# New sequences of steps for all engines, TensorE's filler steps taken out, and SyncE's wait for scattered rows at every load

## The reference

```python
x = x + 0.5 * L0_ffn(layernorm(x))     # top-2 of 8 experts plus a shared one, swiglu
x = x + L0_attn(layernorm(x))          # linear attention, 32 heads, group norm
x = x + 0.5 * L0_ffn(layernorm(x))     # the same routed layer again
x = x + 0.5 * L1_ffn(layernorm(x))     # top-1 of 8 small experts, gelu
x = x + L1_attn(layernorm(x))          # gated recurrence, 8 heads, rope
x = x + 0.5 * L1_ffn(layernorm(x))
```

## Time and profile before

| | |
|---|---|
| median of 3 runs | 1516.47 us (1516.26 to 1516.67) |
| the profiled execution: span | 1515.8 us |
| TensorE busy | 1313.6 us, 87% |
| VectorE busy | 1153.5 us, 76% |
| ScalarE busy | 805.2 us, 53% |
| GpSimd busy | 672.4 us, 44% |
| mean granted TensorE clock | 0.950 of full speed |

### The profile page before, as it was taken

One profiled execution on the slowest core, in us unless ns is written; L12 is line 12 of the kernel. 1 busy time (PEld: TensorE's weight loads), 2 busy tenths in 40 slices (PEclk: granted clock), 3 DMA queues, 4 the chain that ended last, 5 costly groups with the idle time before them and its releaser, 6 DMA issues.

```text
span 1515.8 us, 42570 instructions
## 1 busy us (share of the span) xinstructions
PE 1313.6 (87%) x15621; PEld 1012.9 (67%) x15621; DVE 1153.5 (76%) x3632; ACT 805.2 (53%) x1302; POOL 672.4 (44%) x727
## 2 busy tenths in 40 slices
PE   1566987798978889888898899999999999999998
PEld 0344765576766777666676777777876776767776
DVE  5888788779756698788898587767688778877775
ACT  0344655436534556453566456767666546546662
POOL 0056637785557357767678433221433335210100
PEclk9978999899989999999999999999999988989999
DMA  9002313332143214221333221121110010000000
GB/s 284 0 29 76 104 52 105 90 87 71 52 116 100 66 52 113 70 69 53 107 91 96 71 77 44 40 58 46 43 37 17 22 33 25 17 24 2 9 16 23
DMA packets 128044, 94.30 MB, mean 62 GB/s; under 512 B 15723, under 2 KB 119302, under 8 KB 127590
## 3 DMA queue, kind: packets, MB, share of 16 engines
q1 hardware_dynamic: 108038, 54.17, 12.3%
q0 software_dynamic: 16384, 33.59, 7.6%
q10 hardware_dynamic: 3424, 3.81, 0.8%
HBM read 45.90 MB, written 45.61 MB: 60 GB/s over the span
## 4 chain that ended last, share of the span: by engine, by line
PE 54%; DVE 25%; issue 7%; POOL 6%; ACT 5%; DMA 1%; SPq 0%; POOLq 0%; DVEq 0%; ACTq 0%
PE bank L668 9%; PE bank L725 4%; POOL rows L1605 3%; PE bank L682 3%; PE bank L661 3%; PE bank L702 2%; POOL y_in L1622 2%; PE bank L752 2%; PE bank L530 2%; PE sums L899 2%; PE bank L882 2%; PE sums L913 2%; PE bank L489 2%; DVE heads_store L940 2%; DVE heads_store L1020 1%
## 5 line engine op out<-in xcount | busy, mean ns | idle before, releaser
L1622 POOL DMA_INDIRECT y_in<-ys,r_result x256 | 273.5, 1069 | 120.9 <-issue 69.7
L1605 POOL DMA_INDIRECT rows<-store,r_slot x256 | 264.0, 1031 | 108.9 <-issue 75.8
L668 PE MATMUL bank<-u_xp_odd,w_hi 128*128 128x128 f16 x1216 | 128.6, 224 | 6.9 <-ACT u_xp_odd L1391 6.7
L668 PE MATMUL bank<-u_xp_even,w_hi 128*128 128x128 f16 x1216 | 126.8, 221 | 4.8 <-ACT u_xp_even L1391 4.7
L661 PE MATMUL bank<-r_member,by_expert 128*128 128x512 bf16 x304 | 118.0, 388 | 8.9 <-ACT u_linear_even L1471 3.1
L668 PEld LDWEIGHTS bank<-u_xp_odd,w_hi 128*128 x1216 | 96.5, 100 | 32.4 <-issue 12.0
L668 PE MATMUL bank<-u_xp_odd,w_lo 128*128 128x128 f16 x608 | 117.8, 223 | 0.0
L668 PE MATMUL bank<-u_xp_even,w_lo 128*128 128x128 f16 x608 | 115.7, 220 | 0.0
L668 PEld LDWEIGHTS bank<-u_xp_even,w_hi 128*128 x1216 | 95.1, 98 | 30.1 <-issue 9.2
L1416 ACT ACTIVATE heads_store<-bank,b3s,sc 128x512 f32<-128x512 f32 x64 | 49.4, 775 | 72.3 <-PE bank L530 72.1
L530 PE MATMUL bank<-heads_store,w_hi 128*128 128x512 f16 x256 | 81.8, 403 | 3.8 <-ACT u_linear_odd L1471 1.4
(11 more groups left out here) (348 smaller groups left out, 3797.8 us busy)
## 6 DMA issues: line engine op xcount, KB each, us to landing
u_rows<-rows SPq DMA_DIRECT2D x304, 64.0 KB
ys<-u_y_even SPq DMA_DIRECT2D x38, 256.0 KB
ys<-u_y_odd SPq DMA_DIRECT2D x38, 256.0 KB
x<-x_dram SPq DMA_DIRECT2D x16, 256.0 KB, 7.3
rows<-store,r_slot POOLq DMA_INDIRECT x256
y_in<-ys,r_result POOLq DMA_INDIRECT x256
out_dram<-x SPq DMA_DIRECT2D x16, 256.0 KB
rows<-blank SPq DMA_DIRECT2D x48, 64.0 KB, 1.5
```

Of the source, the lines that this page charges most:

```text
L668: ins = pe.matmul(B[:, of_block[j]], of_expert(wp, e, 2 * part + which), s.xp[:, xp, of_block[j]], start=False, stop=(n == 2 and j == PER_ ...
L1605: pool.indirect_dma_start(row_dram[g], bass.IndirectOffsetOnAxis(route.slot[g][:, i, t:t + 1].bitcast(U32), 0), rows[:, groups[g].first * ...
L1622: pool.indirect_dma_start(fetch.y[i][:, t, k, :], None, y_dram[g], bass.IndirectOffsetOnAxis(route.result[g][:, k, t0 + t:t0 + t + 1].bitc ...
```

## The change

The five strings are replaced. Each has the same letters as before, as many times each, and so the same steps with the same work; only `z`, which stood 462 times in TensorE's string, now stands once, near the end. The first two lines of TensorE's string, before and after:

```diff
         turns = {
             "tensor": (
-                "aazzzzzzzzzzzzzzzzzzzzzzzzzzzzzzzzzzzzzzzzzzzzzzzzzzzzzzzzzzzabbzzzzzzzzbcczzcaabbcaaarrrrbbbcbbbccc"
-                "aaabbabbbaccczccaaarrrrrbbbcccbrrrbaaazzzzzzzzzzzzzzzzarrrrrbbbcccaccaaazzzzzzzzzzzzzzzzzzzuwrrrrrzz"
+                "acbarbabcacaababarbbbbccbarrrrcrarabccbbcbbaabbacrcrcccrababacbcarbrabararbrccacarbbrcrcuwururburwwcau"
...
+                "vvvolvovvllloloooolozlo"
             ),
```

The second edit is in `load_rows`:

```diff
                 firsts = load_numbers(route.row[l][g][0:1, PER_UNIT * u:PER_UNIT * (u + 1)], spare_at + (groups[g].blocks - 1) * BLOCK)
-                if u == 0:
-                    on.wait_ge(scattered[g], 16 * 2 * groups[g].tiles * (l + 1))
-                    on.wait_ge(cleared[g], 16 * (1 + E * (l + 1)))
+                on.wait_ge(scattered[g], 16 * 2 * groups[g].tiles * (l + 1))
+                on.wait_ge(cleared[g], 16 * (1 + E * (l + 1)))
                 if i >= 3:
```

More of the change, by code:

```diff
@@ L396, in build @@
[L396 to L400, removed]
+                "acbarbabcacaababarbbbbccbarrrrcrarabccbbcbbaabbacrcrcccrababacbcarbrabararbrccacarbbcrcuwrurburwwcau"
@@ new lines, in build @@
+                "rwucucwuurcwbucwwbuaububawrbcwuawccuwwwubaaucbaucbcraruwwawurwuarrwauuubwrucbaawaucrwrrwrwracrarraba"
+                "bcwacuwuurawabbaawracucurucrcwaawuubwwrruuawuararuwaucwbucawauwubawbubaruwrabucbcawubwucbcuaubcaabab"
+                "aarcrwwaucwbabbburcaacwcbaawbuawbawacurcacwwaawrruwaccwuuucwauauurawacurawwrarwaauwrwuwuwmuwwruuwuwb"
+                "bbrucwcuwaawuauwuwurbwuuwbuwbwwuubnwbcbwbuuubbbcaucwwcbucbcwcbwwabcbuwcbauubawrrcubwauwcwbacuuwcuaaa"
+                "cuburcaurbcwbccuwbawaabrwccwcbaaaabcuwbcrruwubbwcuwwuubcbcaabacrwccabumrabubacnwacwbcuburawubrbbacca"
@@ new lines, in build @@
+                "bcaacwubwurabucwaabwcuawbcbuaaawarbcrnbuccruabwwuubcbwcrbwacbubawccuwaruauwcbbcawaccrcbraurwabrcbcca"
+                "cawbrubcwauwbraabbauwuacrbcauawlbcwucbubrcuaacbabrwwabcwcwabuuucwarwbcaurcawucuwuwurcwuaurwwcuawrcwa"
+                "auucauauwmwwauruwuwuawwuwruwuuaawwuurmrmmuwmuwnmwnwmntnummttmwnmwutwmttnnwuuottttwutwuowtvwvmnvmuttu"
+                "vtvtmvwmwwnltummttunuvwlnwttnluuunvvmvtlltvnulwumttnmnwtnvmtlowwtuuuvvlwouovmwulvvnwowuuovtotwulnutu"
+                "wntllwowttttowlvvvmlvvwwumvuwnmwtuolouwomluonwmtoutowmuntmutwwttnutnwttmvwmtnomvltnmvntvvtnvttnmmtmt"
@@ L414, in build @@
[L414 to L417, removed]
+                "ababacbccaabraabbrbarbcabcrababccrwccbbacrabrbrcabrbcarcababcrcbabrrrccabrbcruacarrbacrbcbacruuruwwc"
@@ new lines, in build @@
+                "nnottonlffmfotttfftlntftmontfmotolnltmftffmmtotftnlmmtmnmfmfttmlfcftnntttlmanfomfftmoonffftnfnommtft"
+                "nnonbtfftfnlltntamltntmmllnttmofottmftoftlffolffntnlftfntftomfnfltffanlfnttnfmmmmtltnotofttmftnomnmn"
+                "cftttofntffftnflfltmnofmnfftlmftfftmflmtftntlffltoomltlttftlftfbotffmnttnolmlnfannnntltotnoofmmmtmol"
+                "obttmfofmtofttffoftttttblntnottlottltontttcotlltbtonotlalmtlotmtlobtlmntlntlttllttmmnoltcolomlltttoo"
+                "otcoolatloloootlonototlonmcoollb"
@@ L458, in build @@
+                "ulwuwuuuuouuwwwwwuwwwuluwuuwwuuwwwwwulwwuouwwuuuwuuuuwlowluwuwluoluowwluwlulowwuuwllwlwwwluowlooolwl"
+                "ouwlouoloouuwouoouuluowwwulwlooololoooloololloollloollooollllllloololollololllllollollollloolooooolo"
+                "oolooooo"
             ),
```

100 lines of the change are left out of this document (43 added, 57 removed).

## The result

The changed kernel takes 1414.18 us (median of 4 runs, 1407.98 to 1417.71); the kernel before, run beside it, takes 1516.57 us (1516.26 to 1521.25). The ratio is 0.9311, with a 95% interval of 0.9281 to 0.9342. So 102 us went away. 28 us had been predicted, and the range ended at 1462, 48 us above the result: the direction was right, the size far off.

What follows compares the result with a forecast made beforehand. Middle part taken as bound by waits between TensorE and VectorE, last part by TensorE itself. Terms -15 -10 -8 -6 +7 -3 +6 +1 = -28 us; 1515.8 - 28 + 0.7 = 1488.5 us, range 1462 to 1514.

Steps and rivals of the forecast that it cites:

- The fillers, -15 and -10 us: TensorE's filler matmuls taken out: 15 us gained in the last part, 10 us (of 0 to 23) in the middle part.
- The clock, +6 us: TensorE without fillers: 15 us more of half clock at 0.42 cost 6 us, range 0 to 40 us.
- the first rival: Without fillers TensorE falls to 1.2 GHz in the dense part too: slower, 1528 us; chance 0.15.
- TensorE's order, -8 -6 +7 us: Down projection (line 679) gains 8 us, row search (line 608) 6; new waits cost 7; bounds 21 worse to 30 better.
- The named waits: TensorE's waits at the down projection (line 679), 21.3 us, and at the row search (line 608), 9.1 us.
- VectorE's and ScalarE's orders: ScalarE's order: three table loads fewer, 4 us, hidden, so 0; VectorE's order has no term in the sum.
- New waits, 7 us: Waits that TensorE's new order brings and the trace cannot show: 7 us put against that order.
- The third rival: All fillers pay (45 us), waits on lines 679 and 608 (30 us) go with little new: 1464 us; chance 0.16.
- GpSimd, -3 us: GpSimd's first fetch of results comes after 86 scatters instead of 100: 3 us gained, of 0 to 8.
- SyncE, 0: SyncE's edited wait for scattered rows at every unit: six instructions carry it in both programs, so worth 0.
- clock and start: Clock term of 6 us, plus 1 us because the first chunk now meets half clock at the start.

## Why the prediction was wrong, step by step

The sum had 25 us for the fillers and 10 us for the sequences (-8 -6 +7 -3). Measured, taking the fillers out costs 7 us in the old sequences and gives 8 us in the new, and the sequences give 97 to 113 us (1520.1 to 1423.1 with fillers, 1527.7 to 1414.8 without).

- **The fillers, -15 and -10 us:** the step that failed first. Taken out by themselves they changed the time by +7 us (interval of the ratio 1.0015 to 1.0072). I argued that no idle time stood in front of the first matmul behind a run of fillers, so the run must be on the path. But the row shows only that this operand was ready by then; without the run the idle time came back elsewhere (after 60 us TensorE was idle 155 us before, 179 without fillers). Absent idle time behind a filler is no proof that its time can be gained.
- **The clock, +6 us:** for the fillers alone the first rival had the mechanism, but it paid for only part of what the fillers gave back. The granted clock fell from 0.950 to 0.925, half-speed time from 2 x 0.050 x 1516 = 152 to 2 x 0.075 x 1527 = 229 us; at the 0.42 worked out from the earlier trace rows that is an estimated 32 us. An estimated 45 us of fillers gone (at 0.109 us each), 32 us back by the clock and 23.5 us more idle time add up to the 11 us by which the profiled run without fillers is longer. But in the whole change the term has the other sign. The 39 us of busy time between the two kernels without fillers are clock, since the matmuls are the same: by the windows' clocks half-speed time fell by some 87 us, an estimated 37. With its gaps closed TensorE was granted 0.947 and 0.959 in two profiled runs with one filler left.
- **TensorE's order, -8 -6 +7 us:** the step that failed in size, by a factor of ten. The named waits went about as told (the prediction had 13 us left at line 679, there are 8; the row search kept one wait of 2.0). The error is in what a wait is worth: I priced the microseconds in TensorE's own waits on two lines, bounded by their total of 30. The down projections' spacing alone is worth 93 us in the changed kernel, of which 38 are waits at their own line; the rest comes back at other lines, through what VectorE and ScalarE then do later, and as a lower clock.
- **VectorE's and ScalarE's orders:** VectorE's had no term at all, and ScalarE's had 0, from its table loads. These are the two that cost 420 and 247 us when they alone are put back, in the longer session. The prediction read the strings engine by engine, each against the partners' old timing. The gain lies between the strings, and no row of the kernel before holds a price for that.
- **New waits, 7 us:** the one that can be named is that for `u_rows` from DRAM, 10 us (five waits, all of the span), and 7.2 us of it stand in the old sequences too once the fillers are out. The third rival, that the new order covers much more, had the sign and the place; even its 63 us leaned on the fillers for 45, which gave nothing, so that part of it would have been luck.
- **GpSimd, -3 us:** the fetch did start earlier and did wait, 4.88 us. GpSimd's old sequence costs 39 us beside the new ones in the longer session, which is no price of the step alone, but speaks for a term too small. **SyncE, 0:** right, in the instructions and in time.
- **What I had said would show it:** busy time of some 1240 us came as 1241.0, by luck in part: I had taken off the fillers' whole busy time, which overstates them, and had the clock fall. After 60 us it fell by 64.9, of which an estimated 45 are fillers and 15 the higher clock (half-speed time from 152 to 115 us). Idle time after 60 us was to be 194 us and is 110 (1346 less 656.3 and 579.5); 15 us off the last part became 34. Idle time is the number that told the two readings apart. Neither sign of being wrong that I had named (a clock of 0.91 or less, over 215 us idle) came: both watched for too little gain only.
- **Slips in the sums:** the 7 us of new waits are a quarter of the named ones, not a third. The third rival takes 12 us for clock and start where the sum takes 7. The upper end of the clock term, 40 us, is 95 us more of half clock, 1.6 times the 148 and not nearly twice. The runs of the record are 1.6 to 2.1 us longer than their spans, not 0.7. None of these moves the forecast by more than 2 us.

Not settled: which pairs of steps, beside projection and down projection, hold the rest of the gain, and how much of the 420 and 247 us would be left at 1520 us. The kernel with SyncE's wait edited alone wasn't tried, since its instructions are the same.

## What to carry to other kernels

Where engines run fixed sequences, judge an order by pairs: for each step, when the partner's result is there and who needs this one. The wait on one line is no measure of what its step is worth: moving one engine's steps to cure it lost six times the wait here (63 us lost for 10 cured), and the same spacing in sequences laid out for it gave more than twice the waits that it covered (93 us for 38). Before filler work is blamed or praised, take it out alone: with gaps beside it, it cost nothing here, and a denser order gave most of the clock back that it had held (0.947 with one filler, 0.950 with 462 in the old order).

## What the runs showed of the hardware

The same program took 1414.8 us in one session and 1740.1 in another, and the others grew by 17 to 23% likewise. The record has the same chip number for both. In the longer run durations on VectorE are the same (`x<-y_in,r_weight,x` 346 ns in both), but TensorE stands idle with nothing that the profile shows to wait for, and VectorE waits for a releaser that the profile doesn't name (`remote`). TensorE's and VectorE's waits in the changed kernel's longer run:

```profile
PE bank L664 <- issue: 70.1, 78, 6.5
...
PE bank L485 <- issue: 15.8, 22, 2.4
```

```profile
DVE u_linear_odd L1213 <- remote: 38.2, 5, 12.4
DVE u_gated_odd L1213 <- remote: 37.2, 4, 13.8
```

After 60 us TensorE's waits of the kind `issue` are 150.9 us there and 0.9 in the run of 1418 us. Most of the extra time falls on the part before `mid`: old sequences without fillers took 1051 us there instead of 819, and 679 instead of 644 after. The cause stays open; no run here tests one. What follows for measuring is plain: a ratio from such a session (0.9575 for the changed kernel) is another number than that from another (0.9306), and only kernels of one condition can be compared.
